# Depthwise layer of a four-layer image network: another order of the band, residual and input loads and of the third input's normalising

## What is computed

```python
bias = (b77 + b53 + b35)[None, :, None, None]
out = dwconv(x, w77, 3, 3) + dwconv(x, w53, 2, 1) + dwconv(x, w35, 1, 2) \
    + dwconv(dwconv(x, w7w, 0, 3), w7h, 3, 0) + dwconv(dwconv(x, w5w, 0, 2), w5h, 2, 0) + bias
...
x = x + _L2_conv_ref(_gn(x), L2_conv_w77, ...)
```

## Time and profile before

| | us |
|---|---|
| median of 3 runs | 4407.61 (4402.94 to 4409.49) |
| the profiled execution, its time | 4405.0 |
| its span, first to last instruction | 4403.3 |
| depthwise layer in it, first matmul of a group to end of the last | 2818.65 to 3057.7 |

### The profile page before, as it was taken

How to read it: one execution, slowest core, us unless ns; L and a number is a source line. 1 busy time by engine, 2 the same in 40 slices (tenths; PEclk the granted TensorE clock), 3 DMA queues, 4 the chain that set the end, 5 groups by cost and what they waited for, 6 DMA issues and landing times. The chain is left out here.

```text
span 4403.3 us, 53838 instructions
## 1 busy us (share of the span) xinstructions
PE 3966.2 (90%) x17283; PEld 2343.6 (53%) x17283; DVE 3071.4 (70%) x3124; ACT 2265.4 (51%) x3601; POOL 1375.6 (31%) x1108
## 2 busy tenths in 40 slices
PE   6999999999999999749999998455799999999999
PEld 5777777777777677414444443234344444444444
DVE  4757575767676766376777775434888879878878
ACT  2858686767676777533333322222445445544544
POOL 2758575757576767521111100213000000000000
PEclk8999999999999999969999999787899999999999
DMA  4323233333333333110111100647110110110110
GB/s 126 89 76 107 76 104 85 99 90 98 90 94 95 90 98 75 68 57 29 57 43 43 43 29 29 179 136 210 66 43 0 43 43 0 43 43 0 43 43 14
DMA packets 114250, 307.91 MB, mean 70 GB/s; under 512 B 47634, under 2 KB 49250, under 8 KB 104306
## 3 DMA queue, kind: packets, MB, share of 16 engines
q1 hardware_dynamic: 105522, 272.56, 20.1%
q0 software_dynamic: 7504, 24.80, 2.2%
q10 hardware_dynamic: 1008, 7.67, 0.5%
HBM read 203.12 MB, written 101.30 MB: 69 GB/s over the span
## 5 line engine op out<-in xcount | busy, mean ns | idle before, releaser
L417 POOL TENSOR_TENSOR probs_lo<-probs,probs_hi 128x512 fp32r<-128x512 f32 x848 | 1172.0, 1398 | 637.7 <-ACT probs L463 617.8
L530 DVE TENSOR_REDUCE maxima<-m_psum 128x1 fp32r<-128x1024 f32 x512 | 625.3, 1222 | 367.4 <-PE m_psum L706 366.6
L462 ACT ACTIVATE probs_hi<-s_psum 128x512 fp32r<-128x512 f32 x1024 | 614.0, 600 | 382.1 <-PE o_psum L735 220.4
L2376 PE MATMUL psum<-mixes,last_weights 128*128 128x512 f32 x1728 | 751.1, 592 | 0.0
L463 ACT ACTIVATE probs<-s_psum 128x512 f32<-128x512 f32 x1024 | 608.2, 594 | 0.0
L2376 PEld LDWEIGHTS psum<-mixes,last_weights 128*128 128x128 f32 x1728 | 327.5, 190 | 409.8 <-issue 409.8
L719 PE MATMUL s_psum<-q_all,k_hi 128*128 128x512 f32 x1024 | 429.7, 420 | 25.6 <-ACT probs L463 25.4
L735 PE MATMUL o_psum<-probs_lo,v 128*112 128x512 f32 x1024 | 411.9, 402 | 13.4 <-DVE probs_lo L610 6.6
L720 PE MATMUL s_psum<-q_all,k_lo 128*128 128x512 f32 x1024 | 403.6, 394 | 0.0
L730 PE MATMUL o_psum<-probs_hi,v 128*112 128x512 f32 x1024 | 403.3, 394 | 0.0
L2383 PE MATMUL psum<-xp,last_weights 128*128 128x512 f32 x864 | 382.2, 596 | 18.3 <-DVEq L2260 13.3
(11 more groups left out here) (327 smaller groups left out, 6025.4 us busy)
## 6 DMA issues: line engine op xcount, KB each, us to landing
xin<-x SPq DMA_DIRECT2D x17, 1536.0 KB, 6.9
xin<-in_x SPq DMA_DIRECT2D x16, 1536.0 KB, 7.5
k_hi<-k_rows_hi SPq DMA_DIRECT2D x128, 192.0 KB, 3.4
xres<-x SPq DMA_DIRECT2D x16, 1536.0 KB, 7.0
k_rows_hi<-stage_hi SPq DMA_DIRECT2D x48, 256.0 KB, 2.1
k_rows_lo<-stage_lo SPq DMA_DIRECT2D x48, 256.0 KB, 2.3
q_rows_hi<-stage_hi SPq DMA_DIRECT2D x48, 256.0 KB, 2.3
q_rows_lo<-stage_lo SPq DMA_DIRECT2D x48, 256.0 KB, 2.5
```

The lines of the kernel that those rows point to most:

```text
L417: pool.tensor_tensor(probs_lo[:, u % RING, :], probs[:, u % RING, :], as_f32(probs_hi[:, u % RING, :]), ALU.subtract).then_inc(pool_low.ne ...
L462: nc.scalar.activation(probs_hi[:, u % RING, :], s_psum[:, u % 2, :], ACT.Exp, scale=SCALE)
L530: nc.vector.tensor_reduce(maxima[:, g % 2, tile:tile + 1], source, AX.X, ALU.max, negate=True).then_inc(rows_max.next(), 1)
L2376: ins = nc.tensor.matmul(bank, conv_w[:, t, down, factor, m * P:(m + 1) * P], mixes[:, factor, t, down:down + S, :].rearrange("p a b -> p ...
```

## The change

Three edits, all in `depthwise_layer`. Nothing is computed otherwise, and every instruction stays.

```diff
@@ SyncE
+                if s == B:
+                    sp.wait_ge(turned.sem, B)
                 load(s)
             for s in range(2 * B, STEPS):
                 load(s)
@@ GpSimd
-            for t in range(CT):
-                for g in range(GROUPS_T):
-                    load_bands(t * GROUPS_T + g)
-                for k in range(RING * t * (t + 1) // 2, (RING, 3 * RING, STEPS)[t]):
-                    load_res(k)
+            load_bands(0)
+            load_bands(1)
+            pool.wait_ge(turned.sem, B)
+            for n in range(2, 2 * GROUPS_T):
+                load_bands(n)
+                if n < 2 + RING:
+                    load_res(n - 2)
+            load_bands(2 * GROUPS_T)
+            for k in range(RING, 7):
+                load_res(k)
+            load_bands(2 * GROUPS_T + 1)
+            for k in range(7, 12):
+                load_res(k)
+            load_bands(2 * GROUPS_T + 2)
+            load_bands(2 * GROUPS_T + 3)
+            for k in range(12, STEPS):
+                load_res(k)
@@ ScalarE
-                    if t == 1:
-                        for s in range(2 * B + 2 * g, 2 * B + 2 * g + 2):
+                    if t == 1 and g < 2:
+                        for s in range(2 * B + 4 * g, 2 * B + 4 * g + 4):
                             normalise(s)
```

## The result

| | before | changed |
|---|---|---|
| median of 4 runs each, us | 4407.68 | 4377.91 (4375.18 to 4380.56) |
| ratio, 95% interval | | 0.9934 (0.992 to 0.9948) |
| span of the profiled execution | 4403.3 | 4375.8 |

The change makes the kernel 29.8 us faster, against 34 forecast; 4377.91 lies in the range of 4348 to 4394. In the spans the gain is 27.5 us.

The account below looks back on a forecast made before the run. Bound by TensorE's 47.88 us idle ahead of group 8, then its rests for instruction fetch. Groups 5 to 11 gain 32.9, with the start 34: 4405.0 - 34 = 4371, with 2.6 for the median 4373.6 us; range 4348 to 4394.

Parts of the forecast that it names:

- The chain and the cut: Ahead of group 8: bands 8 stood behind residuals, stores and the first turn-back; loading them first removes the 47.8 us stall.
- What comes of ScalarE's order: Tile 1: all turns over about 11 us after group 4's end, turn-backs starting at 2919 instead of 2939.89.
- the cover: Bands 9 out by 2942, bands 10 by about 2962, ahead of groups 9 and 10: 23 us or more to spare.
- Nothing on the path: ScalarE's four normalisings instead of two ahead of its copies: 7.6 us inside a group of 12 to 15, costing nothing.
- What it gives back: Groups 5 to 11: traffic once moved during the stall slows TensorE by 23.6 + 4 us, 117.9 us together.
- The weights' term: Beside groups 5 to 11: ScalarE's 4.1 MB of weights cost 1 us per MB, 4 us, bounds 0 and 1.9 per MB.
- The residuals' and bands' 1.9 us per MB: Beside groups 5 to 11: 12.4 MB on GpSimd's queue at a price from groups 8 and 9, 23.6 us.
- The reading behind the weights' term: SyncE's queue traffic nearly free for TensorE, seen in group 5: 1.05 MB there and 11.8 us.
- Start: Before group 0: step 7's input lands 3 us sooner, bounds 0 and 4.9; net of what was put off, +1.
- Tail: Behind group 11: 36 us of turn-backs 16 to 23 and the weights' transposing, unchanged.
- Full recovery: Rival for groups 5 to 11: nothing is given back, 7 x 12.9 = 90.3 us, time 4344; chance 0.15.
- Slower: Rival: the instruction fetch pays more per MB, balance zero at 4.4; at 5.4 the kernel loses 13 us, 4420; chance 0.04.

## Why the prediction was right, and where it wasn't

- *The chain and the cut.* Bands 8 behind residuals behind stores behind the first turn-back: right. Loading them first removed the hole, and each of the two edits alone removed part of it.
- *What comes of ScalarE's order.* Turn-backs forecast about 11 us behind group 4's end, seen after 11.2. Measured from the start of group 5, which came 1.6 us earlier than before, the later steps were a little ahead of the forecast too: bands 9 at 2935.7 (by 2942), bands 10 at 2958.5 (2962), the last turn-back of tile 1 over at 3002 (3006). That this keeps bands 9 and 10 from becoming the next wait was argued from the cover; the run without ScalarE's edit shows the waits, 8.04 and 8.02 us, and the changed kernel has neither. "Nothing on the path" for the earlier normalisings may have been too good: groups 0 to 4 took an estimated 2 us more with this order (92.5 and 91.4 us with the old start, against 88.7 to 91.4).
- *What it gives back.* For groups 5 to 11 the forecast was 117.9 us. The changed kernel's profile has 122.8, and the version without the start's edits, the same program there, 117.2; before it was 150.0. So the sum is confirmed to about 5 us, and no closer, and its terms less well than their total. The weights' term was too small: "I take 1, 4 us" was 8.4 to 11.5 us, 2.0 to 2.8 us per MB, above even the upper end of 1.9. The residuals' and bands' 1.9 us per MB may be too large: leaving the residuals out gave 1.1 to 1.9. Where the total came out at 117.2, the two errors seem to have cancelled, and that is luck.
- *The reading behind the weights' term.* It took group 5 as proof that queues other than GpSimd's are cheap, and the extra loads on SyncE's queue refute that (2.2 us per MB). The same reading put the stores of SyncE's queue at nothing; they were beside groups 8 and 9 as well, from which the 1.9 was taken, so the price carried part of them unnamed. With the MB of all queues counted, the time above 12.9 us a group is 1.4 us per MB in groups 8 and 9 before (12.8 us, 9.45 MB) and 1.0 to 1.3 in groups 5 to 11 of the changed kernel, the version without the start's edits, and the runs with weights late and without residuals.
- *Start.* Forecast 3 us sooner, net +1 with what was put off. Between the first matmul of the block and group 0 there were 33.4 us before and 32.9 in the changed kernel, half a us. The last input of tile 0 was normalised 29.7 us behind that matmul instead of 30.2, so bands 2 and step 8's input had hardly held it up, and the lower bound of the term, 0, was nearly right; what did make it slow stays open. Groups 0 to 4 took 4.8 us more in that profile, but 2.7 more without the edits too, so about 2 us can be the edits'.
- *Tail.* Forecast unchanged; 37.3 us before, 37.6 now.
- *Sum against measurement.* By these profiles the layer gives 22.4 + 0.5 us, and 30.1 in the profile of the version without the start's edits; the medians say 29.8 and 29.5. The two profiles differ by the scatter of such stretches; the medians, in which the start of the execution scatters as well, agree with each other.
- *Rivals.* Full recovery fell, since groups 5 to 11 took 17.5 us each (16.7 in the version without the start's edits) rather than 12.9. "Slower" needed 4.4 us per MB; the highest price measured by adding, moving or leaving out loads was 2.8. That the fetch would be hidden, as the Trainium skill has it (Runtime: NRT & Kernel Launch, Instruction fetch mechanics), agrees with no run here: quiet groups rest 0.8 us after every 128 matmuls, loaded ones up to 6.31.

## What to carry to other kernels

In an in-order DMA queue, put what the next matmuls need ahead of what waits for the results of the last ones, and make the engine at the head of that chain start earlier: both cut the same chain, and each alone cut only part of it. A stall filled with DMA is not pure loss; once it is gone, price its traffic beside the work, on all queues, here 0.7 to 2.8 us for each MB added, moved or taken away beside a stream of small matmuls. Before believing 5 us between two profiles, compare a stretch that the change can't touch.

## What the runs showed of the hardware

- The same 4.0 MB cost TensorE's stream of small matmuls 2.6 us per MB on GpSimd's queue, 2.2 on SyncE's, and 0.7 on SyncE's as 32 loads in rows of 3.9 KB instead of 16 in rows of 7.8, by one execution each. The halves were issued over 18.87 us and not 8.72, so whether the rows or the pace helped is not shown. That the instructions' fetch stands behind data is the reading that fits: its 16 KB packets came up to 9.2 us apart instead of 3.4 to 3.8; what they waited for is not recorded.
- At a DMA share of 0.95 to 0.97 the cut of the rows brought nothing that could be seen (41.4 us for groups 8 and 9 without it, 43.0 and 42.2 with it).
- The kernels of this study, nearly the same program up to there, reached the first group of this layer between 2812.3 and 2823.5 us. In the pair shown the difference arose within the first 150 us, with granted clocks of 0.86 and 0.92.
